# DLRM forward on one core: splitting the weights through PSUM, more loads in flight, and extra matmuls at the end of the first tile

## Reference

```python
fm = emb_table[arange(26)[None, :], cat_idx]              # (512, 26, 128)
h = relu(dense_x @ Wd1 + bd1)                             # 13 -> 512
h = relu(h @ Wd2 + bd2)                                   # 512 -> 256
dense = relu(h @ Wdf + bdf)                               # 256 -> 128
Z = concatenate([fm, dense[:, None, :]], axis=1)          # 27 vectors a row
S = einsum('bie,bje->bij', Z, Z)
x = concatenate([S[:, iu, ju], dense], axis=-1)           # 351 + 128
x = relu(x @ Wt1 + bt1)                                   # -> 1024
x = relu(x @ Wt2 + bt2)                                   # -> 1024
x = relu(x @ Wt3 + bt3)                                   # -> 512
x = relu(x @ Wt4 + bt4)                                   # -> 256
return sigmoid(x @ Wo + bo)
```

## Time and profile before

| what | value |
|---|---|
| time, median of 3 runs | 179.55 us (178.75 to 179.62) |
| profiled execution, its own time | 179.74 us |
| its span | 177.9 us |
| mean granted TensorE clock | 0.971 |
| PE busy | 161.3 us, 91% |
| PE weight loads | 116.8 us, 66% |
| DVE, ACT busy | 71.1 us, 55.2 us |
| POOL busy | 103.3 us |

### The profile page before, as it was taken

One profiled execution on the slowest core, in us unless ns is written; L12 is line 12 of the kernel. 1 busy time (PEld: TensorE's weight loads), 2 busy tenths in 40 slices (PEclk: granted clock), 3 DMA queues, 4 the chain that ended last, 5 costly groups with the idle time before them and its releaser, 6 DMA issues.

```text
span 177.9 us, 3837 instructions
## 1 busy us (share of the span) xinstructions
PE 161.3 (91%) x1681; PEld 116.8 (66%) x1681; DVE 71.1 (40%) x131; ACT 55.2 (31%) x93; POOL 103.3 (58%) x111
## 2 busy tenths in 40 slices
PE   2999999844999999689999999999999988999983
PEld 1334455332877877578777877777878766788971
DVE  5005258835559822272513034354122165321311
ACT  3376597533437402122202122221112121201110
POOL 4777777777778777777777777777776000000000
PEclk9999999995599999999999999999999999999999
DMA  2899555757977522222221222212221000000000
GB/s 53 326 374 278 161 159 178 224 181 239 338 212 275 152 48 60 54 55 57 46 62 45 59 53 58 55 48 55 52 62 45 15 4 0 0 0 4 0 0 0
DMA packets 6674, 18.18 MB, mean 102 GB/s; under 512 B 2309, under 2 KB 2441, under 8 KB 6530
## 3 DMA queue, kind: packets, MB, share of 16 engines
q1 hardware_dynamic: 3330, 11.12, 18.6%
q0 software_dynamic: 3328, 6.82, 15.2%
HBM read 17.93 MB, written 0.00 MB: 101 GB/s over the span
## 4 chain that ended last, share of the span: by engine, by line
PE 63%; POOL 18%; issue 6%; DVE 5%; DMA 5%; ACT 1%; DVEq 0%
PE mp L448 22%; POOL rows L314 18%; PE mp L417 11%; PE mp L469 8%; PE gp L379 5%; PE gp L369 5%; PE tp L425 5%; DMA rows<-in_emb,row_of 4%; PE mp L510 3%; PE gp L487 3%; DVE xb L729 2%; DVE raw L762 1%; DMA idx<-in_cat_idx 1%; PE gp L391 1%; ACT xth L590 1%
## 5 line engine op out<-in xcount | busy, mean ns | idle before, releaser
L314 POOL DMA_INDIRECT rows<-in_emb,row_of x104 | 102.4, 985 | 33.2 <-issue 29.9
L448 PE MATMUL mp<-w2l,a1h 128*128 128x512 f32 x64 | 26.8, 418 | 0.0
L448 PE MATMUL mp<-w2h,a1h 128*128 128x512 f32 x64 | 26.2, 410 | 0.0
L448 PE MATMUL mp<-w2h,a1l 128*128 128x512 f32 x64 | 25.5, 399 | 0.0
L369 PE MATMUL gp<-ident,rows 128*128 128x128 f32 x104 | 17.2, 281 | 4.6 <-DMA rows<-in_emb,row_of 4.6
L579 ACT COPY zt<-gp 128x512 f32<-128x512 f32 x16 | 9.4, 586 | 38.2 <-PE gp L369 38.1
L369 PEld LDWEIGHTS gp<-ident,rows 128*128 128x128 f32 x104 | 13.2, 144 | 11.3 <-DMA rows<-in_emb,row_of 7.0
L751 DVE TENSOR_TENSOR raw<-mp,bc 128x512 f32<-128x512 f32 x8 | 5.5, 691 | 28.8 <-PE mp L448 28.8
L379 PEld LDWEIGHTS gp<-zt 128*32 128x32 f32 x1024 | 11.7, 112 | 7.1 <-issue 6.7
L379 PE MATMUL gp<-zt 128*32 128x27 f32 x1024 | 13.8, 197 | 0.6 <-DVE zt L723 0.6
L448 PEld LDWEIGHTS mp<-w2h,a1l 128*128 128x128 f32 x64 | 12.1, 189 | 2.9 <-DVE a1l L745 0.9
(11 more groups left out here) (78 smaller groups left out, 233.0 us busy)
## 6 DMA issues: line engine op xcount, KB each, us to landing
w<-in_wt SPq DMA_DIRECT2D x13, 512.0 KB, 4.8
rows<-in_emb,row_of POOLq DMA_INDIRECT x104, 2.8
w<-in_wt SPq DMA_DIRECT2D x3, 468.0 KB
bc<-in_rows SPq DMA_DIRECT2D x1, 1024.0 KB, 7.1
wd_sb<-in_wd SPq DMA_DIRECT2D x1, 512.0 KB, 3.7
w1d<-in_wt SPq DMA_DIRECT2D x1, 512.0 KB, 6.4
bt<-in_rows SPq DMA_DIRECT2D x1, 512.0 KB, 8.9
wdf_sb<-in_wdf SPq DMA_DIRECT2D x1, 128.0 KB, 3.2
```

Of the source, the lines that this page charges most:

```text
L314: pool.indirect_dma_start(out=rows[:, n % RING, :], out_offset=None, in_=emb.rearrange("c v e -> (c v) e"), in_offset=bass.IndirectOffsetO ...
L448: last = pe.matmul(mp[:, h, :], a[:, k, :], w[:, k, cols], start=(k == 0 and part == 0), stop=(k == M1 - 1 and part == 2))
```

## The change

All splits but the last now subtract out of PSUM. Ten whole ones (w1, and w2 chunks 0 to 6) go through `tp` as before. Then come eight pieces of 512 columns: splits 10 to 14 (w2 chunk 7 in two halves, w3 chunks 0 to 2) through `mp[:, 1]`, and 15 to 17 (w3 chunks 3 to 5) through `mp[:, 0]`. Split 18 (w3 chunks 6 and 7, 1024 columns) is subtracted in SBUF. PE waits in `layer_2(0)` at n = 24, where it begins on `mp[:, 1]`, until 15 low parts are made. The loads of w1 and w2 keep four in flight, and two loads of w3 go ahead of `bc`. `turn(t, 4)` moves from behind `transpose_pairs(t + 1)` into `layer_1(t + 1)` at n = 2 for t = 0 and 1. In the first stage `dense_products(7)` moves behind `grams(0, 3)`, and six matmuls whose result nobody reads (`keep_warm`) are put in, the first two behind a wait for DVE's seventh `dense_products_out`. Splits 7 and 8 now stand ahead of `features(0, 6)` on ACT and ahead of `features(0, 7)` on DVE.

```diff
-SPLITS = [("w2", 0), ("w2", 1), ("w2", 2), ("w1", 0), ("w1", 1), ("w1", 2)] + [("w2", k) for k in range(3, M1)] + [("w3", k) for k in range(0, M2, 2)]
-MID_SPLITS, SPLITS_12 = 7, PAIR_CHUNKS + M1
+LOADS = [("w2", 0), ("w2", 1), ("w2", 2), ("w1", 0), ("w1", 1), ("w1", 2)] + [("w2", k) for k in range(3, M1)] + [("w3", k) for k in range(0, M2, 2)]
+LOADS_12 = PAIR_CHUNKS + M1
+IN_FLIGHT = 4
+WHOLE_SPLITS = LOADS_12 - 1
+SPLITS = [(name, k, 0, TOP[1]) for name, k in LOADS[:WHOLE_SPLITS]]
+SPLITS += [("w2", M1 - 1, h * 512, 512) for h in range(2)]
+SPLITS += [("w3", k, 0, 512) for k in range(6)]
+SPLITS += [("w3", 6, 0, 1024)]
+SPLITS_H0, SPLITS_H1 = WHOLE_SPLITS + 5, WHOLE_SPLITS + 8
...
         def split_bank(n):
+            if n >= WHOLE_SPLITS:
+                return mp[:, 1 if n < SPLITS_H0 else 0, :]
...
@@ SP
-            for n in range(2, SPLITS_12):
-                sp.wait_ge(w_in[n - (2 if n < 5 else 1)], 16)
+            for n in range(2, LOADS_12):
+                if n >= IN_FLIGHT:
+                    sp.wait_ge(w_in[n - IN_FLIGHT], 16)
                 load_to_split(n)
             sp.wait_ge(gathered[0][NG - 1], 16 * GROUP_BLOCKS[NG - 1])
+            for n in range(LOADS_12, LOADS_12 + 2):
+                load_to_split(n)
+            sp.wait_ge(w_in[LOADS_12], 16)
...
@@ PE, layer_1
+                        if 0 < t <= LATE:
+                            pe.wait_ge(raw_ready, TURNS * t)
                         pe.wait_ge(xt_hi, t + 1)
...
+                    if n == 2 and 0 < t <= LATE:
+                        turn(t - 1, 4)
                     if n == LAYER_4_IN_1 and 0 < t <= LATE:
                         layer_4(t - 1)
...
                     if n == TURN_1:
                         if t == 0:
-                            pe.wait_ge(w_lo, MID_SPLITS)
+                            pe.wait_ge(w_lo, WHOLE_SPLITS)
...
@@ PE, layer_2
+                    if t == 0 and n == PRODUCTS_2 // 2:
+                        pe.wait_ge(w_lo, SPLITS_H0)
...
@@ PE, first stage
+            def keep_warm(n):
+
+                pe.matmul(mp[:, 1, 0:n], ident[:], w1d[:, 0:n], start=True, stop=True)
...
             grams(0, 2)
-            for m in range(6, 8):
-                dense_products(m)
+            dense_products(6)
+            pe.wait_ge(pre_out, 7)
+            keep_warm(512)
+            keep_warm(512)
             transpose_features(0, 6)
+            keep_warm(512)
             transpose_features(0, 7)
+            keep_warm(256)
             grams(0, 3)
+            dense_products(7)
+            keep_warm(512)
             transpose_pairs(0)
+            keep_warm(256)
             for t in range(LATE):
                 layer_1(t)
                 layer_2(t)
                 layer_3(t)
                 transpose_pairs(t + 1)
-                turn(t, 4)
@@ ACT
                 sc.copy(high, weights).then_inc(w_hi, 1)
-                if n < MID_SPLITS:
+                if n < SPLITS_H1:
                     at_least(sc, w_lo, n)
+                    if n == WHOLE_SPLITS:
+                        sc.wait_ge(raw_ready, 2)
+                    if n == SPLITS_H0:
+                        sc.wait_ge(raw_ready, 3)
                     sc.copy(split_bank(n).bitcast(F32R), weights).then_inc(w_mid, 1)
...
             split_hi(4)
+            split_hi(5)
             features(0, 4)
-            split_hi(5)
             split_hi(6)
+            split_hi(7)
+            split_hi(8)
             features(0, 6)
...
                     if n == TURN_1B:
                         layer_1_hi(t, 1)
                         if t == 0:
+                            for k in range(WHOLE_SPLITS, SPLITS_H0 - 2):
+                                split_hi(k)
                     for g in FEATURES_2[t].get(n, ()):
                         if g % 2 == 0:
                             features(t + 1, g)
+                    if n == PRODUCTS_2 // 2 - 1 and t == 0:
+                        for k in range(SPLITS_H0 - 2, SPLITS_H0 + 1):
+                            split_hi(k)
...
@@ DVE
             dense_products_out(6)
-            dense_products_out(7)
+            split_lo(7)
+            split_lo(8)
             features(0, 7)
             turn_sums(0)
+            dense_products_out(7)
             pairs_lo(0)
-            split_lo(7)
-            split_lo(8)
+            split_lo(9)
...
                         layer_1_lo(t, 1)
                         if t == 0:
-                            split_lo(10)
-                        if t == 0:
-                            for k in range(11, 14):
+                            for k in range(WHOLE_SPLITS, SPLITS_H0):
                                 split_lo(k)
                             ve.wait_ge(rows_sem, 16)
```

More of the change, by code:

```diff
@@ L178, in build @@
         w_mid = sem("w_mid")
-        w_in = [sem(f"w_in{n}") for n in range(len(SPLITS))]
+        w_in = [sem(f"w_in{n}") for n in range(len(LOADS))]
         step_made = sem("step_made")
@@ L239, in split_weights @@
         def split_weights(n):
-            name, k = SPLITS[n]
+            name, k, c, size = SPLITS[n]
             if name == "w1":
@@ L244, in split_weights, with load_of @@
             if name == "w2":
-                return [w[:, k, :] for w in (w2, w2h, w2l)]
-            return [w[:, k:k + 2, :].rearrange("p k n -> p (k n)") for w in (w3, w3h, w3l)]
+                return [w[:, k, c:c + size] for w in (w2, w2h, w2l)]
+            return [w[:, k:k + size // 512, :].rearrange("p k n -> p (k n)") for w in (w3, w3h, w3l)]
         def split_bank(n):
+            if n >= WHOLE_SPLITS:
+                return mp[:, 1 if n < SPLITS_H0 else 0, :]
             rows_of = PC if SPLITS[n][0] == "w1" else P
             return tp[:].rearrange("p k n -> p (k n)")[0:rows_of, :]
+        def load_of(n):
+            name, k = SPLITS[n][0:2]
+            return LOADS.index((name, k - k % 2 if name == "w3" else k))
         block = ctx.enter_context(nc.Block())
@@ L279, in _ @@
             sp.dma_start(bt1[:], bass.AP(tensor=rows_in.tensor, offset=rows_in.offset + ROW1, ap=[[0, P], [1, TOP[1]]])).then_inc(bt1_in, 16)
-            for n in range(2, SPLITS_12):
-                sp.wait_ge(w_in[n - (2 if n < 5 else 1)], 16)
+            for n in range(2, LOADS_12):
+                if n >= IN_FLIGHT:
+                    sp.wait_ge(w_in[n - IN_FLIGHT], 16)
                 load_to_split(n)
             sp.wait_ge(gathered[0][NG - 1], 16 * GROUP_BLOCKS[NG - 1])
+            for n in range(LOADS_12, LOADS_12 + 2):
+                load_to_split(n)
+            sp.wait_ge(w_in[LOADS_12], 16)
             sp.dma_start(bc[:], bass.AP(tensor=rows_in.tensor, offset=rows_in.offset, ap=[[0, P], [1, N_ROWS]])).then_inc(rows_sem, 16)
[L285 to L289, removed]
+            for n in range(LOADS_12 + 2, len(LOADS)):
+                sp.wait_ge(w_in[n - 1], 16)
                 load_to_split(n)
-            sp.wait_ge(w_in[len(SPLITS) - 1], 16)
+            sp.wait_ge(rows_sem, 16)
+            sp.wait_ge(w_in[len(LOADS) - 1], 16)
             sp.dma_start(w4[:].rearrange("p k n -> p (k n)"), wt4).then_inc(w4_in, 16)
@@ L454, in layer_3 @@
                 if t == 0:
-                    pe.wait_ge(w_lo, len(SPLITS))
+                    pe.wait_ge(w_lo, SPLITS_H1)
                 for n in range(PRODUCTS_3):
+                    if t == 0 and n == 3 * SPLITS[-1][1]:
+                        pe.wait_ge(w_lo, len(SPLITS))
                     for g in FEATURES_3[t].get(n, ()):
@@ L649, in _ @@
                             features(t + 1, g)
+                    if n == PRODUCTS_2 // 2 - 1 and t == 0:
+                        for k in range(SPLITS_H0 - 2, SPLITS_H0 + 1):
+                            split_hi(k)
                     if n == TURN_2:
+                        layer_2_hi(t, 0)
                         if t == 0:
-                            split_hi(14)
-                        layer_2_hi(t, 0)
+                            for k in range(SPLITS_H0 + 1, len(SPLITS)):
+                                split_hi(k)
                 for n in range(PRODUCTS_3):
@@ L820, in _ @@
                         if t == 0:
-                            split_lo(14)
+                            split_lo(SPLITS_H0)
                         layer_2_lo(t, 0)
+                        if t == 0:
+                            for k in range(SPLITS_H0 + 1, len(SPLITS)):
+                                split_lo(k)
                 layer_2_sum(t, 1)
```

32 lines of the change are left out of this document (13 added, 19 removed).

## The result

The changed kernel takes 183.06 us (median of four executions, 181.74 to 184.36) and the kernel before, on the same chip, 179.15. The ratio is 1.020 [1.016, 1.024]. The forecast was 180.4 with a range up to 182.7. So it is slower, 2.7 us more than forecast and 0.4 us past the end of the range. Against the kernel before, measured beside it, it is +3.9 us by the medians and +3.6 by the ratio, where the forecast had +0.8. Ratios leave disturbed executions out, and so differ a little from the quotient of the medians in places; the profiled execution of `e13_no_warm` was one, so that only its times are used.

What follows compares the result with a forecast made beforehand. PE was taken as the bound from 44 us on. The terms -1.84 + 2.6 - 1.55 + 1.6 = +0.8 us on the median of 179.55 gave 180.4; own range 179.4 to 181.4, with the rivals 178.2 to 182.7.

Steps and rivals of the forecast that it cites:

- The path through the first stage: Tile 0, splits 7 and 8 ahead of DVE's copy: grams start 1.16 us later, at 40.45; layer 1 at 44.6.
- The loads: First stage: no split waited for a load, so earlier loads gain nothing; they need only be there for splits 7 and 8.
- deeper loads hold back the gathers: Rival, chance 0.07: with four loads in flight, the last gather comes 4 us late, +2 us, 182.4.
- The clock term: Tile 0, clock staying at 1.00: 0.7 us less from grams to layer 1, 2.3 less from there to first turn.
- the old drop: Kernel before: clock at 0.50 from 39.5 to about 49.7 us; its going saves 2.3 us from layer 1 to first turn.
- the clock falls in one of the new holes: Rival, chance 0.20: clock drops where PE idles, 33.9 to 36.0 or 57.9 to 60.5; costs 2.3 us, 182.7.
- The wait in layer 2: Ahead of n = 24 in layer 2, PE waits for split 14: +2.6 us idle, bounds 0 and 3.0.
- The gathers of tile 1: Gathers no longer stretched by DVE's SBUF subtracts, so PE's wait for tile 1's rows goes: -1.55 us.
- The moved turn: Layer 4 waits for ACT's relu behind the later turn: +0.66 and +0.93, together +1.6 us, bounds 0 and 2.0.

Runs made afterwards that it cites:

- e13_no_warm: The changed kernel without the six extra warm matmuls and the wait ahead of them: 184.78 us, ratio 1.028.
- e1_loads_back: The changed kernel with the old waits on the loads of w1 and w2 restored: 182.77 us, ratio 1.020.
- e14_split5_first: The changed kernel with DVE's subtract of split 5 put ahead of its copy of group 5: 182.48 us, ratio 1.012.
- e5_gated: The changed kernel, four loads in flight, those from the seventh on held until tile 0's group 5 gathers have landed: 182.01 us, ratio 1.013.
- e7_gated_turn_back: The kernel of e5_gated with the turn put back behind the transposes of the pairs: 180.73 us, ratio 1.007.
- e2_loads_only: The kernel before with four loads in flight and nothing else: 179.31 us, ratio 0.998.
- e15_no_hole_turn_back: The kernel of e8_no_hole without the gate on the loads, four in flight from the start: 178.24 us, ratio 0.992.
- e8_no_hole: The kernel of e7_gated_turn_back with the split pieces rearranged as in e12_no_hole_only: 177.15 us, ratio 0.986.
- e6_two_in_flight: The changed kernel with two loads in flight instead of four: 183.08 us, ratio 1.019.
- e4_warm_only: The kernel before with extra warm matmuls in the first stage and the eighth dense product moved, nothing else: 179.25 us, ratio 1.002.
- e12_no_hole_only: The changed kernel with split pieces rearranged so PE has no wait ahead of layer 2's second half: 179.93 us, ratio 1.002.

## Why the prediction was wrong

**The path through the first stage: wrong in its start.** The step that failed is the one under "The loads": "Earlier loads gain nothing here; they only must be there for splits 7 and 8". They do gain something, since with the old waits split 8 stands 1.64 us for its weights (`e1_loads_back`), and they delay the gathers beside them: group 5 landed 5.83 us from issue, against 3.57 with the old waits. I had read that no split waits for a load, and never asked what stands beside the loads on the DMA engines. From it, "Split 6 ends at 35.35, so split 7 ends near 37.7 and split 8 near 40.0" took the time of before for a split that was no longer where it had been. The arithmetic behind it held, and so the error went through unchanged, 2.58 us at split 6 and 2.57 at the grams. `e14_split5_first` shows the carrier, DVE's copy ahead of split 5; the timelines of `e5_gated` and `e7_gated_turn_back`, where group 5's rows are in time, show the source.

**The rival "deeper loads hold back the gathers"** is what happened, with the wrong gather. I weighed the last one, which PE needs 2 us later than before, and left those of groups 4 and 5 out as "early". Late rows cost PE little there (it waits 1.23 and 1.76 us for them, and then has to wait for DVE anyway). On DVE they cost more: its copy heads a chain without slack once splits 7 and 8 are in it (without them, `e2_loads_only`: late rows, same time). It should have had more than 0.07. Its price was 2; the rows give 2.57 at the grams, and the times 1.1 (`e15_no_hole_turn_back` against `e8_no_hole`). At a clock of 1.00 `e5_gated` took 180.73 and `e14_split5_first` 180.71, one execution each, against 183.0 and 181.74 after: about 1.7.

**The clock term.** That the old drop goes was right (-2.40 against -2.29). The extra 0.7 between grams and layer 1 measured 4.89 - 4.62 = 0.27. Its size was right all the same: in `e14_split5_first`, `e5_gated`, `e6_two_in_flight`, `e7_gated_turn_back`, `e8_no_hole` and `e15_no_hole_turn_back` the stretch takes 4.05 to 4.27 us. In the changed kernel the last grams come late. DVE's first transpose starts 1.36 us after the grams do, as long as before at the lower clock (1.34), but 1.02 in `e14_split5_first` and 0.81 in `e6_two_in_flight`; from there to layer 1 all of these take 3.24 to 3.26, and before 3.55. Why the grams are slow there is not shown. The warm matmuls are what holds the clock there (`e13_no_warm`, mean 0.972), and they would be worth nothing without the subtracts out of PSUM, since the gathers of tile 1 would take it all back (`e4_warm_only`). The prediction had both halves but didn't say that they need each other.

**The rival "the clock falls in one of the new holes"** came true in some executions. Two of the changed kernel's four stand at 0.991, and they are 1.4 us slower on average than the two at 1.000 (183.74 against 182.37). Where it fell in them no profile shows; in other versions it fell ahead of the warm matmuls or behind the layer 2 hole. For `e14_split5_first` the same step is 1.8 us (182.31 and 182.64 against 180.71). The price of 2.3 was taken from the old drop and was too high; I had given 0.20 to an event that comes in about half of the executions.

**The wait in layer 2** was right in place, cause and size: 2.47 us idle, the stage +2.63. In time it was dearer, 3.1 us in `e12_no_hole_only` and 3.6 in `e8_no_hole`. The clock that no longer falls behind it may account for the rest, but that was not separated.

**The gathers of tile 1** were right: 0.94 up to 68.60, no wait for rows, -1.68 against -1.55. The forecast's place for the last undisturbed one, 64.9, holds too (64.85).

**The moved turn** was right in mechanism: +0.72 and +0.88 in the profile, forecast +0.66 and +0.93. In time it is about 1.3 alone (0.7 to 1.9) and 1.0 to 1.3 taken back, where the forecast had 1.6.

Put together: the late rows (about 1.7) and the clock in half of the executions (about 0.7 on the median) make 2.4 of the 2.7 us that the forecast lacked. The forecast stood on a median of 179.55 and the kernel before took 179.15 beside this one, so as a difference between the kernels it lacked 3.1. Both shares are estimates from one or two executions each. How the two divide in a single execution stays open, since a fall of the clock also moves what comes behind it, and the clean executions are few. It also stays open which of the loads in flight holds back a given gather; the runs changed only depth and order.

## What to carry to other kernels

Before a forecast takes a time of the old trace as the start of a new chain, ask which of the edits can move that start; a transfer that nobody waits for still takes its share from one that somebody does. In an engine's fixed order, a step that waits for data does no harm while there is slack behind it, and sets the end as soon as a tight alternation of two engines follows it, so put work that is ready ahead of it. And a gained clock is only a gain if the next thing that PE waits for comes earlier as well.

## What the runs showed of the hardware

The granted clock differs between executions of one kernel: 0.991 and 1.000 for the changed one, 0.981 to 1.000 for those of `e7_gated_turn_back` that its ratio counts, in whose profiled execution it stayed at 1.00 across idle stretches of 2.04 and 2.48 us. In that of `e14_split5_first` the windows behind its layer 2 hole of 2.47 us show 0.60 and 0.55. Estimated from these differences, one fall costs 1.4 to 1.8 us here.

The last gather of group 5, 128 rows, took 3.57 us from issue to landing with one or two loads of 0.5 MB in flight (`e1_loads_back`; before, PE was on it 3.14 us after issue), 4.12 with two, and with four 5.83 and, in `e15_no_hole_turn_back`, 5.24. It was 6.33 for one of the group behind the gate, issued when the held loads had just been released (`e7_gated_turn_back`, group 6, issued at 32.31). POOL's own time for these gathers didn't change with them (0.94 or 0.95 us).

A gather that meets a DVE subtract with both inputs in SBUF ended 0.81 us after that subtract in each of the four cases named with the result, and took 1.55 to 1.99 us in place of 0.94. Under subtracts out of PSUM it took 0.94 or 0.95.
